# The first 24 of 72 expert tiles run between the links of the last chunk's attention chain, and twelve row buffers stand in for eight

## The chip, the core and the metric

One core of one Trainium2 chip runs the whole kernel. The metric is the time of one execution on the device in microseconds (us), as the median of several runs. The engines of the core are TensorE (PE in the profile, its weight loads PEld), VectorE (DVE), ScalarE (ACT), GpSimd (POOL) and SyncE (SP, which here only issues DMAs). Each works through its own queue strictly in order, and they meet through semaphores.

## The reference

The input is x of 4 x 1024 tokens of 128 channels. Two layers follow, each with attention and a feed-forward part and a layernorm behind each of the four:

```python
x = _layernorm(x + _L0_attn_ref(x, L0_attn_w_qkv, L0_attn_w_out), axis=-1)
x = _layernorm(x + _L0_ffn_ref(x, ...), axis=-1)
x = _layernorm(x + _L1_attn_ref(x, L1_attn_Wq, L1_attn_Wk, L1_attn_Wv, L1_attn_Wo), axis=-1)
x = _layernorm(x + _L1_ffn_ref(x, L1_ffn_W_gate, L1_ffn_W_in, L1_ffn_b_in, L1_ffn_W_out, L1_ffn_b_out), axis=-1)
```

The last one is the part that the change is about. It is a mixture of 8 experts with the 2 best for each token:

```python
gate_logits = jnp.einsum('bpd,de->bpe', x, W_gate)
top_w, top_idx = jax.lax.top_k(gate_logits, K)
top_w = jax.nn.softmax(top_w, axis=-1)
...
for e in range(E):
    h = jax.nn.gelu(jnp.einsum('bpd,dm->bpm', x, W_in[e]) + b_in[e], approximate=False)
    y = jnp.einsum('bpm,md->bpd', h, W_out[e]) + b_out[e]
    out = out + combine[..., e, None] * y
```

## The kernel before

**Stages.** The first attention runs head group by head group until about 540 us (the last of its exponentials starts at 540.2). Then `rear` (L873) runs the rest in chunks of 128 tokens of each of the 4 batches (512 tokens), 8 chunks in all. `body` (L483) is the program of one iteration. It is cut into three parts: "pre" (the output projection of the first attention and its layernorm), "front" (the first feed-forward part) and "rear" (the second attention, its layernorm, the gate and the routing). In iteration `it` the part "rear" is at chunk it-2, the other two are ahead. Iterations 0 and 1 have no rear part; 2 to 7 are a loop; iteration 8 has front and rear, and iteration 9, the last, has the rear part alone (L900 to L910). All engines go through the same written order; a class `Tape` (L353) gives each operation its semaphore values and hands out the 8 PSUM banks in turn (`bank`, L423).

**The end of the rear part.** Behind the last attention step comes `project1(0)` and `project1(1)` (L719: 32 matmuls each, and one add on VectorE at L725), then layernorm 3 (`layernorm`, L458: statistics, variance, a power on GpSimd at L466, the normalization at L469), a transpose and its copy (`turned`, L472), the gate's matmuls (L778), the choice of two experts on VectorE and one exponential on ScalarE (`choose`, L775), the counting matmuls (L810, L812) and `route` (L802), which gives each token and choice a row in the DRAM tensor `rows`, where each expert has a region of its own. `base` holds the next free row of each expert. Then GpSimd issues 8 scatters with one indirect DMA each (L855). The plain result goes to `best` as the residual (L759).

**The experts.** `experts` (L914) follows the last iteration. `tile_table` (L1085) has 16 dependent VectorE steps that find, from `base`, how many tiles of 128 rows each expert has, and for each of 72 tiles (`NTILE`) its expert and its first row. SyncE and ScalarE fill up the last tile of each expert with padding rows, four DMAs each (L924). SyncE waits for all padding and for all scatters (L928 to L931), and then all engines meet at L933. A tile then goes through this pipeline: SyncE reads its row number from the table and loads 128 rows of 130 words (`load`, L949); TensorE transposes (`turn`, L954), VectorE copies the transpose (`take_x`, L986) and the expert's 128 x 640 weights (`take_w`, L991), TensorE has 4 matmul calls (`up`, L959), ScalarE 4 Gelus (`gelu`, L977), TensorE 4 more calls (`down`, L969; an f32 matmul call shows as two matmuls), VectorE scales the bias (`weigh`, L1006) and forms the result (`take_y`, L998), and GpSimd adds it into `best` with one indirect DMA (`back`, L1012). TensorE's order for tile j is turn(j+3), up(j+1), down(j); VectorE's is take_x(j+3), take_w(j+2), weigh(j+1), take_y(j). A row buffer `x_g[k]` is used again when `back` of the tile in it has landed; there are `XG` = 8. The first 8 tiles are written out, the next 56 are a loop of 8 tiles, the last 8 are written out again.

**The tail.** When all of `back` has landed, `best` is read in 8 pieces, the two choices are added, the last layernorm is made and the result is stored (L1040 to L1083).

## Time and profile before

| what | value |
|---|---|
| median of 3 runs | 1412.0 us (1405.41 to 1414.06) |
| profiled execution, its own time | 1410.33 us |
| its span | 1408.2 us |
| mean granted TensorE clock | 0.956 of full speed |
| first scatter of the last chunk starts | 1208.74 us |
| first `back` starts | 1235.14 us |
| last `back` starts | 1377.78 us |

All times from the trace count from the start of the span, which is 2.1 us shorter than the execution's own time. In a timeline row stand the start, the length, the engine, the line and the operation, and in brackets how long the engine had been idle before, with what ended it. A line in a helper, such as L450, L466 or L469, serves several places, so those rows are told apart by their time.

### The profile page before, as it was taken

What the parts mean: (1) busy time and instruction counts of PE and PEld (TensorE: products, weight loads), DVE (VectorE), ACT (ScalarE), POOL (GpSimd) and SP (SyncE); (2) the same over time, 40 slices, a digit from 0 to 9 for tenths busy, and PEclk for the clock granted to TensorE, in tenths of its full rate; (3) what the DMA queues carried; (4) which work ended last, traced back from release to release, by engine and by line L of the source; (5) the groups of instructions that cost most, each with busy time, mean ns of one, the idle gap of its engine ahead of it and who ended that gap; (6) DMA issues with size and microseconds to landing.
All of it is one profiled execution on the core that took longest, in us unless ns stands there. A gap on an engine that the chain in (4) does not pass through costs nothing. (4 is left out here: it accounts for less than half of the span.)

```text
span 1408.2 us, 45352 instructions
## 1 busy us (share of the span) xinstructions
PE 1244.9 (88%) x16752; PEld 764.5 (54%) x16753; DVE 943.2 (67%) x1984; ACT 660.6 (47%) x1321; POOL 518.2 (37%) x509
## 2 busy tenths in 40 slices
PE   7589999999999978999999999999999967299990
PEld 4244444444444433457475656556465635199990
DVE  5668888788877842276867767685868556456664
ACT  4256676666766664242425252333324231055554
POOL 7311211212112211032534436161534344278785
PEclk9789999999999998999999999999999988599995
DMA  6453112121121223030404031131303050244555
GB/s 194 125 190 106 49 47 61 51 58 48 48 61 53 58 75 122 29 76 25 103 16 109 0 84 41 41 84 32 98 7 90 9 156 2 53 58 63 67 63 187
DMA packets 95006, 99.91 MB, mean 71 GB/s; under 512 B 16096, under 2 KB 76640, under 8 KB 94752
## 3 DMA queue, kind: packets, MB, share of 16 engines
q1 hardware_dynamic: 75808, 81.47, 20.6%
q0 software_dynamic: 13568, 12.13, 5.5%
q10 hardware_dynamic: 5504, 4.46, 1.0%
q8 instruction: 99, 1.62, 0.5%
q14 instruction: 27, 0.22, 0.0%
HBM read 49.84 MB, written 27.87 MB: 55 GB/s over the span
## 5 line engine op out<-in xcount | busy, mean ns | idle before, releaser
L1487 DVE TENSOR_REDUCE arena<-banks 128x4 f32<-128x512 f32 (+3 forms) x336 | 343.7, 1068 | 94.7 <-PE banks L1256 90.3
L1422 ACT ACTIVATE arena<-banks 128x512 f32<-128x512 f32 x576 | 304.9, 603 | 166.0 <-PE banks L1256 160.9
L1256 PE MATMUL banks<-arena 99*32 99x512 bf16 (+7 forms) x6144 | 337.0, 331 | 30.3 <-DVE arena L1487 12.1
L1256 PEld LDWEIGHTS banks<-arena 96*32 96x32 bf16 (+1 forms) x6144 | 151.4, 97 | 191.2 <-ACT arena L1422 69.3
L450 PE MATMUL banks<-arena,h 128*128 128x512 f32 x512 | 226.7, 593 | 2.4 <-DVEq L395 1.0
L1624 POOL TENSOR_SCALAR_AFFINE_SELECT arena<-arena 128x512 f32<-128x512 f32 x128 | 79.9, 637 | 383.1 <-ACT arena L1422 369.7
L1323 PE MATMUL banks<-arena 128*32 128x512 f32 (+3 forms) x1536 | 153.7, 490 | 11.2 <-POOL arena L1624 11.0
L450 PEld LDWEIGHTS banks<-arena,h 128*128 128x128 f32 x512 | 94.7, 190 | 110.0 <-issue 105.2
L598 ACT ACTIVATE arena<-banks,sh 128x512 f32<-128x512 f32 x64 | 44.0, 687 | 215.9 <-PE banks L450 215.9
L1015 POOL DMA_INDIRECT best<-arena x72 | 117.4, 1630 | 42.8 <-issue 25.8
L466 POOL TENSOR_TENSOR arena<-arena 128x4 f32<-128x4 f32 x23 | 23.4, 1017 | 267.0 <-DVE arena L464 267.0
L637 POOL TENSOR_TENSOR arena<-arena,qdec 128x512 f32<-128x512 f32 x64 | 87.6, 1391 | 63.5 <-DVE arena L541 43.1
L982 ACT ACTIVATE arena<-banks,b_in 128x128 f32<-128x128 f32 x288 | 82.3, 369 | 61.2 <-PE banks L964 55.2
L1256 PE MATMUL banks<-mask_qk,identb 128*32 128x128 bf16 x2048 | 102.9, 222 | 1.9 <-issue 1.9
L586 POOL TENSOR_TENSOR arena<-arena,kdec 128x512 f32<-128x512 f32 x64 | 84.5, 1345 | 32.8 <-ACT arena L577 17.6
L712 DVE SCALAR_TENSOR_TENSOR arena<-arena,bdec,banks 128x128 f32<-128x128 f32 x256 | 69.0, 342 | 30.6 <-PE banks L699 30.6
L855 POOL DMA_INDIRECT rows<-arena x64 | 63.5, 993 | 49.3 <-DVE arena L829 25.8
L450 PE MATMUL banks<-h,arena 128*128 x576 | 80.0, 282 | 1.4 <-ACT arena L982 0.8
L964 PE MATMUL banks<-arena 128*128 128x128 f32 x576 | 78.9, 281 | 2.1 <-DVE arena L995 2.1
L708 ACT COPY arena<-banks 128x512 f32<-128x512 f32 x64 | 34.4, 590 | 89.7 <-PE banks L699 89.7
L964 PEld LDWEIGHTS banks<-arena 128*128 128x128 f32 x576 | 71.6, 195 | 3.4 <-issue 2.7
L450 PEld LDWEIGHTS banks<-h,arena 128*128 128x128 f32 x576 | 69.8, 191 | 3.6 <-issue 2.3
(172 smaller groups left out, 1761.5 us busy)
## 6 DMA issues: line engine op xcount, KB each, us to landing
arena<-arena SPq DMA_DIRECT2D x160, 128.0 KB, 2.3
arena<-k_parts SPq DMA_DIRECT2D x96, 96.0 KB
arena<-rows SPq DMA_DIRECT2D x72, 65.0 KB
arena<-q_parts SPq DMA_DIRECT2D x64, 64.0 KB
k_parts<-arena SPq DMA_DIRECT2D x24, 128.0 KB, 3.2
q_parts<-arena POOLq DMA_DIRECT2D x24, 128.0 KB, 3.0
arena<-q_parts SPq DMA_DIRECT2D x32, 96.0 KB
best<-arena SPq DMA_DIRECT2D x12, 256.0 KB, 3.0
```

The lines of the kernel that those rows point to most:

```text
L450: ins = nc.tensor.matmul(dst, l, r, start=(n == 0), stop=(n == len(pairs) - 1), skip_group_check=True)
L586: lambda: nc.gpsimd.tensor_tensor(v_dec[:, n % 2, kp, :, :].rearrange("p g (i d) -> p g i d", i=4), v_nat[:, n, 2 * kp:2 * kp + 2, :].rear ...
L637: lambda: nc.gpsimd.tensor_tensor(q_dec[:, n % 2, 4 * kp:4 * kp + 4, :, :], q_all[:, 4 * kp:4 * kp + 4, n * P:(n + 1) * P].rearrange("p i ...
L712: tp.do("dve", f"state{n}", [f"attn{n}", f"grow{n}"], lambda: last(nc.vector.scalar_tensor_tensor(out=state[:, 2 * pr:2 * pr + 2, blk, :], ...
L964: ins = nc.tensor.matmul(banks[:, 2 + k % 2, m * P:(m + 1) * P], w_now[:, k % 4, m * P:(m + 1) * P], x_gT[:, k % 4, :], start=True, stop=T ...
L982: ins = nc.scalar.activation(h_g[:, k % 2, m * P:(m + 1) * P], banks[:, 2 + k % 2, m * P:(m + 1) * P], ACT.Gelu, bias=b_in[:, bass.ds(x, 1 ...
L1015: nc.gpsimd.indirect_dma_start(out=best, out_offset=bass.IndirectOffsetOnAxis(x_g[:, k, C:C + 1].bitcast(U32), 0), in_=y_g[:, k, :], in_of ...
L1256: ins = nc.tensor.matmul(dst[c:c + 32, :], lhs[:, c:c + 32], rhs, start=start, stop=stop, skip_group_check=True)
L1323: done.append(nc.tensor.matmul(pv_bank[32 * h:32 * h + 32, lo:lo + n], va[p][:, kt, h, :], pe_[:, s % NSLOT, at:at + n], start=(g in (0, 3 ...
L1422: nc.scalar.activation(pe_[:, s % NSLOT, :], score[s % NBANK], ACT.Exp, scale=SCALE0)\
L1487: nc.vector.tensor_reduce(mx[:, 1 if k0 else 0, qt, hs[0]:hs[-1] + 1], src, AX.X, ALU.max)\
L1624: ins = nc.gpsimd.affine_select(out=v, in_=v, compare_op=ALU.is_ge, fill=0.0, base=0, pattern=[[0, v.shape[1]], [1, P]], channel_multiplie ...
```

## The change

- `XG` goes from 8 to 12. `h_g` moves to the memory of `k_all`, since the row buffers now fill `q_all`.
- The first 24 tiles (`AHEAD`) are planned by a new function `plan_table` of 19 dependent VectorE steps in iteration 8, behind its layernorm 3. It uses `base` after six chunks and counts only tiles that are full by then. Their loads need the scatters of the first six chunks alone.
- The steps of a tile are in a class `Tiles`. In the last iteration, behind `project1(0)`, `begin` issues on SyncE the 12 first loads, on TensorE three transposes and on VectorE three `take_x`, two `take_w` and one `weigh`. From there the rear part has only PSUM banks 6 and 7 (`narrow`), and TensorE waits first for the users of the other six.
- Four tiles are run by `slot(0)` to `slot(3)` between the links of the rear part: most of slot 0 between the power and the normalization of layernorm 3, slot 1 behind the normalization, slot 2 behind the transpose, slot 3 between `choose` and `route`. Tiles 4 to 23 are written out behind the rear part.
- `tile_table` now has 21 steps for the other 48 tiles, in three parts behind tiles 5, 7 and 9 on VectorE. All eight padding DMAs are on SyncE, two each behind its steps for tiles 6 to 9. The waits for all scatters, for the padding and for the table are at tile 24, and the meeting of all engines is gone. SyncE's order is load(j+12) in the slot of tile j.
- The first `back` waits for the zeroing of `best` and for the plain result of the last chunk (L759).
- The other 48 tiles are a loop of 12 tiles that runs three times, and 12 written out.

```diff
-XG = 8
+XG = 12
+AHEAD = 24
+LATER = NTILE - AHEAD
...
@@ body
             project1(0)
+            if tp.tiles:
+                tp.tiles.begin(tp)
...
+            if tp.tiles:
+                tp.tiles.first_up()
-            layernorm(tp, 3, "res3_1", res, x3, [("scatter7", 1), ("stored", 1)])
+            layernorm(tp, 3, "res3_1", res, x3, [("scatter7", 1), ("stored", 1)], lambda: slot(0, "sp", "pe", "act", "dve"))
+            slot(0, "y", "pool")
+            slot(1, "sp", "pe", "act", "dve")
+            if tp.me == "dve" and tp.eng is not None and isinstance(it, int) and it == NITER - 2:
+                tp.wait(("base", 1))
+                tp.wait(("outproj", 1))
+                plan_table()
...
             tile2(2)
             tp.part = "rear"
+            slot(1, "y", "pool")
+            slot(2, "act")
             turned(tp, 3, x3, x3T, [("gate", 1), "up_b3"])
...
+            slot(2, "sp", "pe", "dve", "y", "pool")
             choose()
+            slot(3, "sp", "pe", "act", "dve", "y", "pool")
...
@@ Tiles
+                def load(J, k):
+                    if isinstance(J, int) and XG * J + k == AHEAD:
+                        e.wait_ge(s_line["scat"], 16 * TOPK * B * (NITER - 2))
+                        e.wait_ge(s_pad, 16 * 2 * NE)
...
+                def back(J, k):
+                    if isinstance(J, int) and XG * J + k == 0:
+                        e.wait_ge(s_zeroed, 16 * (NZERO - NT // 512))
+                        e.wait_ge(s_line["out"], 16 * NITER)
...
+            def begin(self, tp):
+                e, me = self.e, self.me
+                owed = tp.narrow()
+                if me in ("sp", "act", "dve"):
+                    tp.wait("scores3")
+                    tp.wait("qdec31")
...
+                if me == "sp":
+                    e.wait_ge(s_line["scat"], 16 * TOPK * B * (NITER - 4))
+                    for j in range(XG):
+                        self.do("load", j)
+                if me == "pe":
+                    for n in owed:
+                        tp.wait(n)
+                    for j in range(3):
+                        self.do("turn", j)
...
@@ experts
+            table_parts = tile_table() if me == "dve" else iter(())
+            for j in range(4, AHEAD):
+                tiles.slot(j, ("sp", "pe", "act", "dve", "y", "pool"))
+                if j in (5, 7, 9):
+                    next(table_parts, None)
+                if me == "sp" and j in (6, 7, 8, 9):
...
-            e.sem_inc(s_off, 1)
-            e.wait_ge(s_off, 10)
```

## Rows read from the trace of the kernel before

**Rows 1.** The chain of waits, ahead of the tiles and behind them.
```profile
1213.57 6.93 issue
...
1377.78 3.23 DMA best<-arena
```

**Rows 2.** The costliest groups of the page, line 1015.
```profile
L1015 POOL DMA_INDIRECT best<-arena x72 | 117.4, 1630 | 42.8 <-issue 25.8
```

**Rows 3.** Line 1015 by itself (ns least/median/most), then its timeline.
```profile
L1015 POOL DMA_INDIRECT best<-arena x72: 1549/1602/1870, 1235.1 to 1377.8; - x72
...
1235.14 1.67 POOL L1015 DMA_INDIRECT best<-arena  x1 [15.97 <-DVE arena L1002]
...
1267.40 1.55 POOL L1015 DMA_INDIRECT best<-arena  x1 [1.05 <-DVE arena L1002]
```

**Rows 4.** Timeline of TensorE, the transposes of two tiles that follow each other.
```profile
1235.68 0.27 PE L957 MATMUL banks<-ident,arena 128*128 128x128 f32 x1
...
1237.57 0.27 PE L957 MATMUL banks<-ident,arena 128*128 128x128 f32 x1
```

**Rows 5.** The chain of waits, a back that lands and the load that follows it.
```profile
1256.98 3.37 DMA best<-arena
1260.51 3.02 DMA arena<-rows
```

**Rows 6.** Line 855 in the last chunk, the eight scatters (ns).
```profile
L855 POOL DMA_INDIRECT rows<-arena x8: 957/970/1264, 1208.7 to 1218.2; - x8
```

**Rows 7.** Timeline of VectorE: the gap in iteration 8, and the table's first and last step.
```profile
1132.40 0.19 DVE L781 COPY arena<-banks 128x32 f32<-128x32 f32 x1 [7.69 <-PE banks L778]
...
1207.83 0.17 DVE L1101 CAST arena<-arena 128x8 uint32<-128x8 f32 x1
...
1214.14 0.20 DVE L1117 CAST arena<-arena 128x72 uint32<-128x72 f32 x1
```

**Rows 8.** Timeline of SyncE's queue: four padding DMAs, then four loads.
```profile
1209.04 4.54 SPq L924 DMA_DIRECT2D rows<-in_padding  x4
1221.37 3.65 SPq L952 DMA_DIRECT2D arena<-rows  x4
```

**Rows 9.** Timeline of TensorE: one gate, a projection, the last gate, a tile's up.
```profile
1131.41 0.95 PE L778 MATMUL banks<-wgate,arena 128*128 128x8 f32 x8
...
1194.47 1.95 PE L450 MATMUL banks<-wo1s,arena 128*128 128x128 f32 x16
...
1202.23 1.87 PE L778 MATMUL banks<-wgate,arena 128*128 128x8 f32 x8 [0.68 <-ACTq L395]
...
1233.89 1.06 PE L964 MATMUL banks<-arena 128*128 128x128 f32 x8
```

**Rows 10.** Timeline of VectorE, the links of the last chunk's rear part.
```profile
1192.34 0.42 DVE L725 TENSOR_TENSOR arena<-banks,arena 128x256 f32<-128x256 f32 x1 [1.58 <-PE banks L450]
...
1198.24 0.17 DVE L464 TENSOR_SCALAR arena<-arena 128x4 f32<-128x4 f32 x1
1199.56 1.11 DVE L469 TENSOR_SCALAR arena<-arena 128x128 f32<-128x128 f32 x4 [1.15 <-POOL arena L466]
...
1206.61 0.23 DVE L816 TENSOR_TENSOR arena<-banks,arena 128x72 f32<-128x72 f32 x1
```

**Rows 11.** Timeline of VectorE in the tiles, from a take_x to the next weigh.
```profile
1286.58 0.28 DVE L989 COPY arena<-banks 128x128 f32<-128x128 f32 x1
...
1287.82 0.28 DVE L1010 TENSOR_SCALAR arena<-arena 128x128 f32<-128x128 f32 x1
```

**Rows 12.** Timeline of ScalarE: the exponential, then the first Gelus of the tiles.
```profile
1205.53 0.21 ACT L790 ACTIVATE arena<-arena 128x4 f32<-128x4 f32 x1 [3.34 <-DVE arena L788]
...
1230.21 1.28 ACT L982 ACT_TABLE_LOAD   x1 [24.48 <-PE banks L964]
1231.51 2.18 ACT L982 ACTIVATE arena<-banks,b_in 128x128 f32<-128x128 f32 x8
```

**Rows 13.** Busy time in one stretch: span, PE, PEld, DVE, ACT, POOL, granted TensorE clock, DMA share, GB/s.
```profile
1202.00:1207.00 5.00, 2.38 (x17) 2.19 (x17) 2.48 (x24) 0.39 (x2) 0.00 (x0) 0.50 0.11 33
```

More of the change, by code:

```diff
@@ L365, in __init__ @@
                 self.part = None
+                self.tiles = None
+                self.two = None
             def wait(self, need):
@@ L421, in do, with narrow @@
                 self.where[name] = (line, self.count[line])
-            def bank(self):
+            def narrow(self):
+                last = {}
+                for k in range(len(self.held)):
+                    last[k % 8] = self.held[k]
+                self.two = [last[6], last[7]]
+                self.turn = 0
+                return [n for b in range(6) for n in last[b]]
+            def bank(self):
+                if self.two is not None:
+                    if self.part not in self.live:
+                        return None, banks[:, 6, :], []
+                    self.turn ^= 1
+                    return -1 - self.turn, banks[:, 6 + self.turn, :], self.two[self.turn]
                 k = len(self.held)
@@ L486, in body, with slot @@
             c = it - 2
+            def slot(j, *who):
+                if tp.tiles:
+                    tp.tiles.slot(j, who)
             tp.part = "pre"
@@ L893, in rear, with run @@
             body(dry)
-            def run(it, live):
+            def run(it, live, tiles=None):
                 tp = Tape(e, me, it, live, dry)
+                tp.tiles = tiles
                 body(tp)
@@ L909, in rear @@
                 e.dma_start(w_dn, a["w_dn"].rearrange("e p m c -> p e (m c)")).then_inc(s_experts, 16)
-            run(NITER - 1, {"rear"})
-            experts(e, me)
-        def experts(e, me):
-            if me == "dve":
-                tile_table()
-            if me in ("sp", "act"):
-                e.wait_ge(s_tab, 1)
-                for g in range(NE):
-                    if g % 2 == (me == "act"):
-                        r = e.value_load(table[0:1, 2 * NTILE + g:2 * NTILE + g + 1], min_val=0,
+            tiles = Tiles(e, me)
@@ new lines, in experts @@
+        def experts(e, me, tiles):
+            table_parts = tile_table() if me == "dve" else iter(())
[4 more added lines that the diff above has]
+                if me == "sp" and j in (6, 7, 8, 9):
+                    if j == 6:
+                        e.wait_ge(s_tab, 1)
+                    for g in range(2 * j - 12, 2 * j - 10):
+                        r = e.value_load(table[0:1, 2 * LATER + g:2 * LATER + g + 1], min_val=0,
@@ L949, in load @@
-            def load(J, k):
-                r = e.value_load(at(NTILE + XG * J + k), min_val=0, max_val=NE * REGION + NE * P - P)
-                wait(s_back[k], 16 * J)
-                e.dma_start(x_g[:, k, :], rows[bass.ds(r, P), :]).then_inc(s_xg[k], 16)
-            def turn(J, k):
-                e.wait_ge(s_xg[k], 16 * (J + 1))
-                wait(s_xt, XG * J + k - 1)
-                nc.tensor.transpose(banks[:, k % 2, 0:P], x_g[:, k, 0:C], ident[:, :]).then_inc(s_tp, 1)
-            def up(J, k):
-                e.wait_ge(s_xt, XG * J + k + 1)
-                e.wait_ge(s_w1, XG * J + k + 1)
-                wait(s_gelu, XG * J + k - 1)
-                for m in range(4):
-                    ins = nc.tensor.matmul(banks[:, 2 + k % 2, m * P:(m + 1) * P],
-                                           w_now[:, k % 4, m * P:(m + 1) * P],
-                                           x_gT[:, k % 4, :], start=True, stop=True, skip_group_check=True)
-                ins.then_inc(s_up, 1)
@@ L1012, in back @@
-            def back(J, k):
-                e.wait_ge(s_y, XG * J + k + 1)
-                e.sem_inc(s_hold, 1)
-                nc.gpsimd.indirect_dma_start(
-                    out=best, out_offset=bass.IndirectOffsetOnAxis(x_g[:, k, C:C + 1].bitcast(U32), 0),
-                    in_=y_g[:, k, :], in_offset=None, compute_op=ALU.add).then_inc(s_back[k], 16)
-            chain = {"sp": [(load, 0)], "pe": [(turn, 3), (up, 1), (down, 0)], "act": [(gelu, 0)],
-                     "dve": [(take_x, 3), (take_w, 2), (weigh, 1), (take_y, 0)], "pool": [(back, 0)]}[me]
@@ L1022, in experts, with group @@
             NJ = NTILE // XG
-            for fn, ahead in chain:
-                for k in range(ahead):
-                    fn(0, k)
-            def tiles(J, final):
+            def group(J, final):
                 for k in range(XG):
-                    for fn, ahead in chain:
+                    for fn, ahead in tiles.chain:
                         if k + ahead < XG:
@@ L1033, in tiles @@
                             fn(J + 1, k + ahead - XG)
-            tiles(0, False)
-            with e.Fori(1, NJ - 1) as J:
-                tiles(J, False)
-            tiles(NJ - 1, True)
+            with e.Fori(AHEAD // XG, NJ - 1) as J:
+                group(J, False)
+            group(NJ - 1, True)
             NC = 2 * B
```

257 lines of the change are left out of this document (181 added, 76 removed).

## The prediction

> **What bounds the kernel now.** I read the chain of waits first. Between the last step of the rear part at about 1208 us and the first `back` at 1235.14 it holds no matmul work of weight: a table, 6.93 us of nothing but waiting for scatters [rows 1], and then the pipeline of the first tile. Behind that stand the tiles, and behind them a tail from 1377.78 on. The group of line 1015 says what bounds the tiles: 72 indirect DMAs of 1.63 us mean with the engine idle 0.30 us at least between two of them, that is 1.93 us for a tile on GpSimd [rows 2, 3]. TensorE needs nearly as much: two transposes that follow each other start 1.89 us apart with no idle row between them [rows 4]. The 72 starts run from 1235.14 to 1377.78, so the real pitch is 142.64 / 71 = 2.01 us [rows 3]. The 0.08 above GpSimd's own 1.93 are places where it waits for its feed, such as the 1.05 us at 1267.40 [rows 3]: a load that could go only when the `back` of eight tiles earlier had landed [rows 5].
>
> So two things are to be had: the 26.4 us from the first scatter at 1208.74 [rows 6] to the first `back`, in which GpSimd has only 8 scatters to issue, and some of the 0.08 us a tile.
>
> **The plan, its loads and the memory.** `plan_table` has 19 steps where the table of before took 1207.83 to 1214.34 for 16 [rows 7], most of them wider. 19 x (6.51 / 16) = 7.7 us is the upper end; its widest steps have 256 elements where the old ones had 576, and I take 5. VectorE is idle 7.69 us at that place of iteration 8 [rows 7], so it costs 0; above the cover it would cost 0 to 1. SyncE has nothing else to do there: its 12 loads at 1.10 us (3.65 us for four, less one issue) [rows 8] can start once the scores of the last step have left `q_all`, some 8 us before TensorE wants the first. Free too.
>
> **What the four tiles cost the rear chain.** Let T be the end of `project1(1)`, 1196.42 before [rows 9]. TensorE now waits for the add behind `project1(0)`, done at 1192.76 [rows 10], since its bank is one of the six handed over, and then has three transposes, the third behind a VectorE copy: some 1.3 us. T becomes 1197.8, which is 1.4 later.
>
> From there, in us behind T. Before: variance done 2.0, normalized 4.3, gate done 7.7, `place` behind the counting matmuls at 10.2, first scatter 12.3 [rows 6, 9, 10].
> - VectorE has a take_x, a take_w and a weigh in the place where it waited 1.15 us for the power [rows 10]. They take 1.52 us in the tiles, from 1286.58 to 1288.10 [rows 11]. Normalized at 4.7.
> - ScalarE needs the Gelu table, 1.28 us [rows 12], between up(0) and the first Gelu: gelu(0) ends at 3.7 and gelu(1) at 4.8, at half of 2.18 us each [rows 12].
> - TensorE, in order: up(0), turn(3), up(1), down(0) to 4.7, turn(4), up(2), down(1) to 6.8, at 0.95 us for an up or a down that is not held up (half of the 1.89 [rows 4]). Only then the transpose of x3, whose input lay ready at 4.7: done 7.2, copied 7.9.
> - turn(5), up(3), down(2) to 9.2, and the gate to 10.2. It takes 0.95 us at the full 2.4 GHz; before it took 1.87, with a granted clock of 0.50, that is 1.2 GHz, after a stretch in which TensorE had had one transpose since T [rows 9, 13]. The tiles keep TensorE busy there, so I take 0.95.
> - The choice up to the exponential is 1.4 us, as from 1204.10 to 1205.53 [rows 9, 12]: the exponential ends at 11.8. Before, slot 3 was not there. Now gelu(3) is behind the exponential, with the Gelu table once more: 13.2, done 14.4; down(3) 15.3. The counting matmuls are behind down(3), with VectorE behind take_y(3): 15.9. From `place` to the first scatter it is 2.1 us as before, 1206.61 to 1208.74 [rows 6, 10].
>
> First scatter at T + 18.0 instead of T + 12.3, so 5.7 + 1.4 = 7.1 us later: 1215.8. The lower end is 3: only what waits of `begin` and one Gelu with its table. The upper end is 14.7: TensorE at 1.2 GHz all through, where an up of 1.06 takes about twice that, 1.9 us more for each of four tiles. I take 7.1, since TensorE has no gap of over 3 us in this plan.
>
> Here the Trainium skill speaks against the change: "ScalarE: Activation LUTs", section "What ACT_TABLE_LOAD costs", gives a switch of table set 2.66 us, of which 1.28 are the load and the rest a drain. The trace has the load at 1.28, and the first Gelu starts 0.02 us behind it [rows 12]. By the page the two switches on the chain would add 2 x 1.38 = 2.8 us, which I leave out.
>
> **What the tiles gain.** GpSimd has `back` 0 to 3 done before the scatters: 0 when the plain result has landed (about T + 8), 3 at T + 15.7 to 17.3, just free for the first scatter. Then 8 scatters, mean 1.04 + 0.30 [rows 6], 10.7 us: `back` 4 starts at 1226.5. By then TensorE is six tiles ahead, so GpSimd has work without a gap, and its queue alone sets the pace: 67 x 1.93 = 129.3. The last `back` starts at 1355.8 instead of 1377.78: **22.0 us earlier**. The tail stays.
>
> Does the feed hold? Twelve buffers give 12 x 1.93 = 23.2 us for a round that takes, from the start of a `back`, 3.4 + 3.0 to the landed load [rows 5], four TensorE slots of 1.89 and a take_y, together some 15. The three parts of the table add about 2 us each on VectorE between tiles 5 and 10, while GpSimd is still at the scatters: covered by the six tiles. On SyncE each of the slots 6 to 9 has two padding DMAs at 1.30 behind its load of 1.10 [rows 8], 3.7 us against a pitch of 1.93, so it falls 7 us behind. The tightest load, of tile 22, is then issued by 1249.9 and its result is there at about 1260, while GpSimd wants it at 1226.5 + 18 x 1.93 = 1261.2. It holds by 1 us; were it missed, by a microsecond or two once.
>
> Bounds of the pace: 1.85 (1.55 + 0.30, the least) makes it 5.4 us better; the pitch of before, 2.01, makes it 5.3 worse. I take 1.93, the mean of all 72 rows.
>
> **The sum.** The profiled execution has 1410.33 us; less 22.0 it is 1388.3. The median shown, 1412.0, is 1.7 above the profiled one, so I predict 1390.0 for the median. The forecast's own range is 1380 to 1398.
>
> **The rivals.**
> 1. *The pitch does not fall.* The feed sets it and not GpSimd: TensorE at 1.89 is only 0.04 below, and 2.01 is what a tile took [rows 3, 4]. For it: GpSimd's idle time is 25.8 / 70 = 0.37 us a row and not 0.30 [rows 2], the longer waits left out. Against: twelve buffers and a lead of six tiles, which at 0.08 a tile would last to the end. Gain 22.0 - 5.3 = 16.7: 1395.
> 2. *GpSimd is held up more.* Its rows range from 1.55 to 1.87 [rows 3]. If all were 1.87, because it now never rests and always meets VectorE's copies, 67 x 0.24 = 16 us are lost: gain 6, 1406. Against: 70 of 72 rows had tile work on VectorE beside them and the mean is 1.63. "SBUF — State Buffer", section "Who interferes with whom", of the Trainium skill says that VectorE in a two-port mode and GpSimd lock each other out for a whole instruction; the spread of 0.32 us over rows of one shape agrees with that, and no row here says how often it will fall so.
> 3. *The slots do not fit the chain*, the slower side. In each slot every engine does a tile's step ahead of the next link, and the one waits for the other. Run one after the other, a tile's steps are 11 us (from the first load's issue at 1221.37 to the first `back` at 1235.14 are 13.8 [rows 3, 8], of which I give the load some 2.5); four of them, 44 us, would put the first scatter at 1252.7 and the end 15 us later than before: 1427. It decides from 29 us of delay on (7.1 + 22.0). Against: steps of two tiles are always in the queue, and TensorE's part of four tiles is 7.6 us.
> 4. *It does not do what it says*: `back` 0 to 3 come only behind the scatters, since the plain result is late or GpSimd is at the wrong place. Then four more of 1.93 stand behind them: gain 14.3, 1397.
> 5. *Better:* the chain loses only 3 us, or the pace is 1.88: gain 26, 1386 and below.
>
> **How the numbers follow.** Forecast 0.57, rival 1 0.16, rival 2 0.09, rival 3 0.03, rival 4 0.05, rival 5 0.10. A measurement of this kernel tells about 1%, 14 us, from no change. Faster by over 1% (below 1397.9) are the forecast, rival 5, nearly all of rival 1 and half of rival 4: 0.84. Slower by over 1% is rival 3 alone: 0.03. Within 1%: 0.13. From 1377 to 1400 lie the forecast, rivals 1 and 5 and most of rival 4; it leaves out rivals 2 and 3.
>
> **What would show it.** Right: four rows of `back` ahead of the first scatter of the last chunk; the first scatter at about 1216; 8 scatters in 10 to 11 us; then 68 rows of `back` with an idle time of 0.30 nearly throughout and a last start near 1356; the gate at 0.95 us; two table loads more on ScalarE; no 6.93 us of pure waiting. Wrong: a first scatter behind 1225, gaps on GpSimd over 1 us at tiles 20 to 24 (SyncE's padding), a mean `back` above 1.75, or TensorE at half clock between 1192 and 1216.

## The result, and the profile after

| | before | after |
|---|---|---|
| median | 1411.22 us (7 runs, 1405.41 to 1414.06) | 1401.75 us (7 runs, 1398.41 to 1403.32) |
| profiled execution, its span | 1410.33, 1408.2 us | 1403.32, 1401.6 us |
| A, the add behind the projection in iteration 8 (VectorE) | 1120.48 | 1123.89 |
| first scatter of the last chunk | 1208.74 = A + 88.3 | 1221.43 = A + 97.5 |
| last `back` starts | 1377.78 = A + 257.3 | 1371.43 = A + 247.5 |

The ratio of the mean times is 0.9937, with a 95% interval of 0.9915 to 0.9958. By the medians the change is 9.5 us faster where 22 were forecast, and 1401.75 is outside the range. A lies ahead of everything that the change touches in the timeline, and from one profiled execution to the next it lies anywhere from 1115.5 to 1123.9 us with the same code ahead of it, so I count from A. By that the last `back` is 9.8 us earlier, and not 22.0.

GpSimd in the last chunk, from its timeline; line 1066 is `back` and line 906 the scatters. The first row shown is `back`(0), the second `back`(3); dots stand for rows left out:

```profile
1209.07 1.64 POOL L1066 DMA_INDIRECT best<-arena  x1 [4.29 <-DVE arena L1050]
...
1219.39 1.73 POOL L1066 DMA_INDIRECT best<-arena  x1 [4.94 <-POOLq L407]
1221.43 1.00 POOL L906 DMA_INDIRECT rows<-arena  x1 [0.30 <-issue]
...
1230.56 1.08 POOL L906 DMA_INDIRECT rows<-arena  x1 [0.30 <-issue]
1231.95 1.60 POOL L1066 DMA_INDIRECT best<-arena  x1 [0.30 <-issue]
...
1236.87 1.77 POOL L1066 DMA_INDIRECT best<-arena  x1 [1.45 <-DVE arena L1050]
...
1249.44 1.56 POOL L1066 DMA_INDIRECT best<-arena  x1 [2.70 <-DVE arena L1050]
...
1257.23 1.62 POOL L1066 DMA_INDIRECT best<-arena  x1 [0.50 <-issue]
...
1371.43 1.55 POOL L1066 DMA_INDIRECT best<-arena  x1 [0.30 <-issue]
```

Four tiles are done ahead of the scatters, as planned. The scatters take 10.5 us, from 1221.43 to 1231.95. Against the prediction the last `back` is 12.2 us late (A + 247.5 for A + 235.3), and these rows split that into three:
- first scatter at A + 97.5 where the sum gave 95.3: 2.2 us (the scatters themselves gave 0.2 back);
- tiles 4 to 13, from 1231.95 to 1257.23: 25.3 us for nine steps, where nine of 1.93 are 17.4: **7.9 us**. GpSimd waits for VectorE's take_y (line 1050) before tiles 6, 8, 9, 10, 11 and 12;
- the other 58 steps, 114.2 us, at 1.97 and not 1.93: 2.3 us.

The group of line 1066 answers to [rows 2]. A `back` costs what it did; the idle time before it hardly fell:

```profile
L1066 POOL DMA_INDIRECT best<-arena x72 | 116.3, 1615 | 41.4 <-issue 22.8 <-DVE arena L1050 13.7 <-POOLq L407 4.9
```

The timeline of TensorE answers to [rows 9] and goes on to the waits. Lines: 481 down, 825 the gate, 857 and 859 the counting, 1005 turn, 1012 up.

```profile
1210.49 0.96 PE L825 MATMUL banks<-wgate,arena 128*128 128x8 f32 x8
...
1211.44 1.06 PE L1012 MATMUL banks<-arena 128*128 128x128 f32 x8
1216.13 2.07 PE L481 MATMUL banks<-h,arena 128*128 x8 [3.63 <-ACT arena L1030]
...
1218.07 0.46 PE L859 MATMUL banks<-arena 128*128 128x64 bf16 x8
...
1223.21 1.06 PE L481 MATMUL banks<-h,arena 128*128 x8
...
1224.21 1.06 PE L1012 MATMUL banks<-arena 128*128 128x128 f32 x8
1225.10 1.14 PE L481 MATMUL banks<-h,arena 128*128 x8
...
1230.92 2.05 PE L1012 MATMUL banks<-arena 128*128 128x128 f32 x8 [4.57 <-issue]
1232.79 2.07 PE L481 MATMUL banks<-h,arena 128*128 x8
```

The gate has its 0.96 us. Then come two gaps, each followed by matmuls of twice the length: 3.63 us ahead of down(3) and 4.57 us ahead of up(8). What follows the first is at 1.2 GHz, by the granted clock (0.50) of that stretch, the row that answers to [rows 13]:

```profile
1216.00:1220.00 4.00, 3.87 (x25) 3.81 (x26) 1.65 (x10) 1.03 (x4) 0.61 (x1) 0.50 0.08 21
```

In the first gap TensorE waits for ScalarE, which has the exponential, its way back to the Gelu table and gelu(3), as [rows 12] had them for the tiles:

```profile
1212.86 0.21 ACT L837 ACTIVATE arena<-arena 128x4 f32<-128x4 f32 x1 [1.99 <-DVE arena L835]
1213.56 1.28 ACT L1030 ACT_TABLE_LOAD   x1 [0.49 <-issue]
1214.85 2.18 ACT L1030 ACTIVATE arena<-banks,b_in 128x128 f32<-128x128 f32 x8
```

At the second gap, VectorE and ScalarE (line 1050 take_y, 1239 the first step of the table's first part, 1043 take_w, 1030 the Gelus) have these rows:

```profile
1227.07 0.35 DVE L1050 SCALAR_TENSOR_TENSOR arena<-banks,arena 128x128 f32<-128x128 f32 x1 [2.79 <-PE banks L481]
1227.33 0.16 DVE L1239 CAST arena<-arena 128x8 uint32<-128x8 f32 x1
...
1230.32 0.49 DVE L1043 COPY arena<-arena 128x640 f32 x1 [0.67 <-issue]
...
1235.72 0.35 DVE L1050 SCALAR_TENSOR_TENSOR arena<-banks,arena 128x128 f32<-128x128 f32 x1 [4.71 <-PE banks L481]
```
```profile
1231.51 1.14 ACT L1030 ACTIVATE arena<-banks,b_in 128x128 f32<-128x128 f32 x4 [6.86 <-remote]
1235.95 1.14 ACT L1030 ACTIVATE arena<-banks,b_in 128x128 f32<-128x128 f32 x4 [3.30 <-PE banks L481]
```

Read them pairwise with TensorE's. down(5) is over at 1224.27 (1223.21 + 1.06), yet take_y(5), which VectorE stands idle for, starts at 1227.07. up(7) is over at 1225.27, and its Gelu, with ScalarE idle for 6.86 us, starts at 1231.51. down(6) is over at 1226.24, and take_y(6) starts at 1235.72, VectorE having been idle for 4.71 us. So what TensorE has done by its records reaches the other engines 3 to 10 us later. It is not the waiting engine that is slow: gelu(8) waits for down(6) as well, as the user of its buffer, and it starts on ScalarE at 1235.95, 0.23 us behind take_y(6) on VectorE. Nor is it the loading of program code, as far as the trace shows: the instruction queues moved no packet between 1218 and 1236 us. Behind the late take_y(5) stand a table part and take_w(8), and behind that up(8): the gap of 4.57 us.

### The profile page after: what moved, and what is told of

The parts are those of the page before. It is cut to its first block and busy times, and to the rows that moved or that the text cites. A ratio compares the mean times of both kernels' runs of the same rounds, so it can differ in the third digit from the quotient of the medians.

```text
span 1401.6 us, 45150 instructions
## 1 busy us (share of the span) xinstructions
PE 1246.2 (89%) x16752; PEld 767.7 (55%) x16753; DVE 951.1 (68%) x2008; ACT 662.7 (47%) x1323; POOL 516.9 (37%) x509
## 5 line engine op out<-in xcount | busy, mean ns | idle before, releaser
L1635 DVE TENSOR_REDUCE arena<-banks 128x4 f32<-128x512 f32 (+3 forms) x336 | 343.4, 1066 | 92.8 <-PE banks L1404 88.4
L481 PE MATMUL banks<-h,arena 128*128 x576 | 83.0, 290 | 5.9 <-ACT arena L1030 5.3
L1012 PEld LDWEIGHTS banks<-arena 128*128 128x128 f32 x576 | 74.3, 202 | 11.1 <-issue 10.8
L481 PEld LDWEIGHTS banks<-h,arena 128*128 128x128 f32 x576 | 74.0, 201 | 7.3 <-issue 6.8
```

Source lines behind the costliest of these rows:

```text
L481: ins = nc.tensor.matmul(dst, l, r, start=(n == 0), stop=(n == len(pairs) - 1), skip_group_check=True)
L1012: ins = nc.tensor.matmul(banks[:, 2 + k % 2, m * P:(m + 1) * P], w_now[:, k % 4, m * P:(m + 1) * P], x_gT[:, k % 4, :], start=True, stop=T ...
L1635: nc.vector.tensor_reduce(mx[:, 1 if k0 else 0, qt, hs[0]:hs[-1] + 1], src, AX.X, ALU.max)\
```

## The experiments

Each group of runs below is one session on one chip; groups 1 and 5 had the same chip, groups 2, 3 and 4 one each of their own; that of the first result is not on record. The unedited changed kernel, repeated as a control, does not have one time: 1401.75 at first, then 1391.06 (group 2), 1397.13 (group 3), 1390.46 (group 4) and 1393.12 us (group 5). "Nine steps" is the time from `back`(4) to `back`(13); where tiles start behind the scatters it is the first `back` behind them and the nine that follow. "Later pitch" is the mean step from there to the last `back`. These and the times behind A come from the one profiled execution of each row, which need not lie at its median.

| run | median us | ratio to before, 95% | first scatter | nine steps | later pitch | last `back` |
|---|---|---|---|---|---|---|
| before | 1411.22 | | A + 88.3 | 17.5 | 2.02 | A + 257.3 |
| the change | 1401.75 | 0.9915–0.9958 | A + 97.5 | 25.3 | 1.97 | A + 247.5 |
| e1 unedited | 1390.9 (one run) | | A + 97.4 | 18.4 | 1.97 | A + 240.4 |
| e2 buffers alone | 1404.09 | 0.9971–0.9997 | A + 87.7 | 17.2 | 1.98 | A + 253.8 |
| e3 table in seven parts | 1394.13 | 0.9875–0.9920 | A + 97.7 | 17.2 | 1.98 | A + 240.0 |
| e4 tiles behind scatters | 1396.70 | 0.9903–0.9941 | A + 87.4 | 20.8 | 2.02 | A + 243.7 |
| e5 unedited | 1391.06 | 0.9853–0.9895 | A + 97.5 | 18.4 | 1.97 | A + 240.4 |
| e6 Gelu first | 1386.61 | 0.9812–0.9846 | A + 93.2 | 17.5 | 1.97 | A + 236.0 |
| e7 = e6 + e3 | 1389.62 | 0.9825–0.9870 | A + 94.9 | 17.2 | 1.98 | A + 237.4 |
| e8 = e4 + seven parts | 1396.21 | 0.9866–0.9910 | A + 89.3 | 22.3 | 1.97 | A + 244.4 |
| e9 unedited | 1397.13 | 0.9883–0.9927 | A + 97.3 | 24.9 | 1.97 | A + 246.9 |
| e10 Gelu first | 1395.70 | 0.9879–0.9939 | A + 93.6 | 25.2 | 1.97 | A + 243.2 |
| e11 half of down | 1391.59 | 0.9838–0.9890 | A + 95.6 | 22.3 | 1.87 | A + 236.9 |
| e12 unedited | 1390.46 | 0.9856–0.9913 | A + 97.1 | 18.7 | 1.97 | A + 240.4 |
| e13 scatters later | 1398.67 | 0.9919–0.9964 | A + 122.3 | 17.3 | 1.91 | A + 245.5 |
| e14 filled, 32 | 1393.91 | 0.9875–0.9917 | A + 99.3 | 16.8 | 1.98 | A + 241.6 |
| e15 tiles behind scatters | 1397.54 | 0.9894–0.9942 | A + 88.3 | 20.1 | 2.04 | A + 245.4 |
| e16 unedited | 1393.12 | 0.9851–0.9905 | A + 96.0 | 18.4 | 1.97 | A + 239.0 |
| e17 scatters later | 1398.16 | 0.9885–0.9937 | A + 122.6 | 17.2 | 1.90 | A + 245.3 |
| e18 filled, 12 | 1391.23 | 0.9823–0.9882 | A + 96.9 | 16.9 | 1.97 | A + 238.4 |

### Group 1: the parts of the change

e1 is the changed kernel as it is.

> The changed kernel once more, with nothing edited, to see whether the gaps behind the scatters are a property of it. In its first profile tiles 4 to 13 took 25.3 us on GpSimd where nine pitches of 1.93 are 17.4, and two up/down groups of TensorE signalled up to 6 us after their matmuls in the record. Theory (the VectorE queue starves the feed): 1399 to 1403 us and 24 to 27 us for those nine pitches again. Rival (a chance stall of TensorE in that one execution): the late signals are gone and the nine pitches take 20 us or less.

It gave 1390.9 us in its one execution, 10.9 below the first result, and the table shows where: the nine steps take 18.4 us and not 25.3. First scatter and later pitch are the same. So the largest of the three losses is not in the program alone.

e2, the kernel before with twelve row buffers and nothing else:
```diff
-XG = 8
+XG = 12
-        x_gT, h_g = reuse([P, 4, P]), reuse([P, 2, 512])
+        x_gT, h_g = reuse([P, 4, P]), k_all
```

> The kernel of before with 12 row buffers and nothing else. If the 0.08 us a tile above GpSimd's own 1.93 come from the loads that wait for a buffer, the pitch falls from 2.01 to 1.93 to 1.95 and the time by 4 to 5 us (ratio 0.996 to 0.997). If they come from somewhere else (TensorE at 1.89 with VectorE's steps between), the pitch stays at 1.98 to 2.01 and the ratio is 0.998 to 1.001.

The pitch behind the first ten tiles falls from 2.02 to 1.98, the last `back` comes 3.5 us sooner, and the ratio is 0.9984. That is the second of the two outcomes expected: the buffers do not bring GpSimd to 1.93. They are worth 2.2 us by the ratio of the means (0.4 to 4.1) and 3.5 by the medians, and their pitch ends where that of the changed kernel ends, at 1.97 to 1.98.

e3, a piece of three steps of the table behind each of tiles 4 to 10:
```diff
-                if j in (5, 7, 9):
+                if 4 <= j <= 10:
```

> The changed kernel with the 21 steps of the table in seven parts of three behind tiles 4 to 10, not in three parts behind tiles 5, 7 and 9. The work is the same. Theory (a part of 2 us at a time on VectorE holds take_w and take_y of the next tile, and the feed starves): the nine pitches fall from 25 to 20 to 22 us and the ratio to before from 0.994 to 0.990. Rival (the gaps come from TensorE at 1.2 GHz and late, or from SyncE's padding): no change, 0.993 to 0.995.

Against e1 the nine steps are 1.2 us shorter and the last `back` 0.4 us earlier: nearly nothing. The 25 us that the expectation starts from did not occur in e1, so it was not tried as written. Where completions come in time, the parts of 2 us on VectorE are nearly covered, as was forecast.

e4, all 24 planned tiles behind the scatters, nothing between the links:
```diff
-                if tp.tiles:
-                    tp.tiles.slot(j, who)
+                pass
-            for j in range(4, AHEAD):
+            for j in range(0, AHEAD):
```
(`begin` and `first_up` move to the end of `body`.)

> The changed kernel with nothing between the links: begin, first_up and tiles 0 to 3 stand behind the route of the last chunk, and the tiles run from there on. The plan, the 12 buffers and the table parts stay. By the sum of the prediction the four slots gain 4 x 1.93 = 7.7 us of GpSimd's queue and cost 7.1 to 9 us of delay of the first scatter, so this kernel is as fast as the changed one or up to 2 us faster from that alone; and since TensorE builds up its lead over GpSimd while the scatters go out, with the table inside that lead, up to 8 us more come back: ratio 0.985 to 0.993. Rival (the slots are where the gain of the change is): 0.996 to 1.000.

The chain keeps its old length (A + 87.4), the first `back` comes with no wait behind the last scatter, at 1214.57, and the end is only 3.3 us behind e1's. So most of the change's gain, 13.6 of 16.9 us by the last `back`, is what it does behind the scatters (tiles planned ahead, the buffers, the table off the path); the four tiles between the links add the rest. That profile is the fastest of e4's four runs. By the medians of group 4, where e15 repeats it, the parts are 11.1 of 18.1 us. The ratio of 0.9922 is in the range expected (0.985 to 0.993), but the expectation also took e4 to be as fast as the change or faster, and it is slower. The four tiles between the links cost the chain 10 us and bring four tiles of 1.9 plus TensorE's lead. Without the lead GpSimd waits, at tiles 8 and 10 most:

```profile
1233.17 1.71 POOL L1064 DMA_INDIRECT best<-arena  x1 [2.33 <-DVE arena L1048]
...
1239.63 1.56 POOL L1064 DMA_INDIRECT best<-arena  x1 [2.70 <-DVE arena L1048]
```

### Group 2: the exponential and the Gelu table

e5, unedited, five rounds:

> The changed kernel unedited, now timed in five rounds beside the kernel before on one chip. Its first seven runs gave 1401.75 us against 1411.22 (0.9937), one run on another chip 1390.9 against 1407.6 (0.988). If the late signals of TensorE belong to that first chip or execution, this is 0.986 to 0.990 here, with the nine pitches behind the scatters at 18 to 19 us. If they belong to the kernel and come and go, the runs spread over 1390 to 1403 and the ratio is about 0.991.

1391.06 us. The nine steps again take 18.4 us. The same place in GpSimd's timeline, to be laid beside the first fence:

```profile
1225.02 1.60 POOL L1066 DMA_INDIRECT best<-arena  x1 [0.31 <-DVE arena L1050]
...
1241.25 1.71 POOL L1066 DMA_INDIRECT best<-arena  x1 [1.10 <-DVE arena L1050]
```

And TensorE's down(5), up(8) and down(7), then VectorE's take_y(5):

```profile
1216.31 1.06 PE L481 MATMUL banks<-h,arena 128*128 x8
...
1221.23 1.26 PE L1012 MATMUL banks<-arena 128*128 128x128 f32 x8 [1.86 <-issue]
1222.28 2.00 PE L481 MATMUL banks<-h,arena 128*128 x8
```
```profile
1217.40 0.35 DVE L1050 SCALAR_TENSOR_TENSOR arena<-banks,arena 128x128 f32<-128x128 f32 x1 [0.27 <-PE banks L481]
```

down(5) is over at 1217.37, and take_y(5) starts at 1217.40. The gap ahead of up(8), which waits for the take_w behind the table part, is 1.86 us where it was 4.57; down(7) behind it still takes 2.00 us. The order of the program, the gap ahead of down(3), the half clock behind it and the table part are the same in both executions; what differs is how late TensorE's completions arrive.

e6 puts gelu(3) ahead of the exponential on ScalarE:
```diff
+            slot(3, "act")
             choose()
-            slot(3, "sp", "pe", "act", "dve", "y", "pool")
+            slot(3, "sp", "pe", "dve", "y", "pool")
```

> ScalarE does the Gelus of tile 3 ahead of the exponential of the gate and not behind it; nothing else is moved. The prediction gave that place 1.3 us for the second table load and 1.1 for the Gelus, behind which down(3) and the counting matmuls wait, and the trace shows 3.63 us of TensorE idle there and half clock after it. Theory (this wait is the largest single link of the 12 us by which the scatters come later): first scatter 4 to 5 us earlier, time 3 to 5 us below the changed kernel on the same chip. Rival (the feed behind the scatters takes it back): first scatter earlier, time within 1 us of the changed kernel.

ScalarE's timeline: gelu(3), the exponential's table (1.28 us, over well before its input is there), the exponential, and the Gelu table again, now for tile 4:

```profile
1204.03 1.14 ACT L1031 ACTIVATE arena<-banks,b_in 128x128 f32<-128x128 f32 x4 [0.40 <-PE banks L1013]
1205.19 1.28 ACT L837 ACT_TABLE_LOAD   x1
1207.00 0.21 ACT L837 ACTIVATE arena<-arena 128x4 f32<-128x4 f32 x1 [0.53 <-DVE arena L835]
1208.00 1.28 ACT L1031 ACT_TABLE_LOAD   x1 [0.79 <-PE banks L481]
```

First scatter 4.3 us sooner than in e5, last `back` 4.4 us sooner, median 4.5 us lower, and the ratio's interval lies below that of e5: 1386.61 us, the lowest median of all.

e7 (e6 with the table in seven parts) and e8 (e4 with it):

> e6 with the table in seven parts of three steps behind tiles 4 to 10. If the parts of 2 us held the feed, this is 1 to 3 us below e6, since with earlier scatters there is less lead to hide them; if they did not, it is equal to e6.

> e4 (no tile between the links) with the table in seven parts of three steps behind tiles 0 to 6. In e4 GpSimd waited 8 us in all at tiles 6 to 11, each time for VectorE. Theory (the table's steps in VectorE's queue): those waits fall to under 2 us and the time 4 to 7 us below e4, so that running behind the chain beats running between its links: 1389 to 1392. Rival (TensorE has simply no lead there): the waits stay and so does the time.

Neither gained: 1389.62 us against e6's 1386.61, with intervals that overlap, and 1396.21 against 1396.70 for e4, which ran in the other session. In e8 the waits of 2.3 and 2.7 us at tiles 8 and 10 are gone, but 0.5 to 1.6 us stand at each of tiles 1 to 8, 7.7 us in sum against 8.4 in e4. Spreading the table moves the waits and does not shorten them.

### Group 3: the late completions again

> The changed kernel unedited for the third time, five rounds. It gave 0.9937 of before in its first seven runs and 0.9874 in e5, with a profile that has late TensorE signals of up to 6.1 us at tiles 5 to 7 in the first case and none in e1 and e5. If the slower result belongs to one chip or one session, this is 0.986 to 0.990 again unless it meets the same chip. If it comes and goes in the kernel, some of these runs lie at 1398 to 1403 and others at 1390.

> e6 once more in another session beside the unedited changed kernel, as the version that may beat it: 3 to 5 us below it again if the place of the Gelus of tile 3 is what counts; within 1 us if e6 was a matter of that session.

Here the losses of the first profile are back, for both kernels: nine steps of 24.9 and 25.2 us. In e9, VectorE's take_y and ScalarE's Gelu at the same tiles:

```profile
1223.64 0.35 DVE L1050 SCALAR_TENSOR_TENSOR arena<-banks,arena 128x128 f32<-128x128 f32 x1 [3.32 <-PE banks L481]
1232.27 0.35 DVE L1050 SCALAR_TENSOR_TENSOR arena<-banks,arena 128x128 f32<-128x128 f32 x1 [4.69 <-remote]
```
```profile
1229.46 1.14 ACT L1030 ACTIVATE arena<-banks,b_in 128x128 f32<-128x128 f32 x4 [8.65 <-remote]
```

e10 keeps e6's earlier first scatter (3.7 us, A + 93.6) and its earlier last `back` (3.7 us), though the medians are only 1.4 us apart here, with intervals that overlap.

One suspect for the late completions falls with e10: TensorE's gap ahead of down(3) and the half clock behind it. e10 has no such gap. From 1198 us until turn(10) is over at 1216.57 TensorE never stands idle for more than 1.70 us, and it has its full clock until 1218 (granted clock 1.00). Its rows of up(7) and down(6), the clock, gelu(7), and take_y(6) (the lines are one higher here):

```profile
1214.51 1.06 PE L1013 MATMUL banks<-arena 128*128 128x128 f32 x8
1215.41 1.06 PE L481 MATMUL banks<-h,arena 128*128 x8
...
1198.00:1218.00 20.00, 15.14 (x133) 14.18 (x132) 13.30 (x64) 12.06 (x34) 11.54 (x10) 1.00 0.29 51
...
1222.85 1.14 ACT L1031 ACTIVATE arena<-banks,b_in 128x128 f32<-128x128 f32 x4 [7.94 <-PE banks L1013]
...
1227.05 0.35 DVE L1051 SCALAR_TENSOR_TENSOR arena<-banks,arena 128x128 f32<-128x128 f32 x1 [6.88 <-PE banks L481]
```

up(7) is over at 1215.57 and down(6) at 1216.47, and their followers start 7.3 and 10.6 us later. So neither the gap ahead of down(3) nor a half clock behind it is needed for the late completions. The scatters are still beside them. In the first profile, in e9 and in e10 take_y(6) starts 14.3 us behind the start of the first scatter, while the recorded end of down(6) lies 4.8, 4.3 and 3.7 us behind it. This points at the scatters and does not show that they are the cause. (e11, below, also has late completions, at tiles 6 to 8.)

e11 leaves out two of down's four matmul calls, so that half of the hidden columns are missing from the result:
```diff
-                         for m in range(4)]).then_inc(s_down, 1)
+                         for m in range(2)]).then_inc(s_down, 1)
```

> The changed kernel with two of the four down matmul calls of each tile, so the second half of the hidden columns is left out of the result. TensorE's pace falls from 1.89 to about 1.45 us a tile, GpSimd's work is untouched. Behind tile 13 the changed kernel takes 1.97 us a tile where GpSimd alone would need 1.91 (1.61 + 0.30). If that 0.06 is TensorE's and the lead that it lacks, the pitch falls to 1.91 to 1.93 and the time by 4 to 6 us; if it is GpSimd's own (code, DMA), the pitch stays at 1.96 to 1.98 and only the first tiles gain, 1 to 2 us.

It takes 1391.59 us, 5.5 below e9. The pitch falls to 1.87, lower than the 1.91 to 1.93 expected, with GpSimd's `back` at a median of 1.551 and a mean of 1.57:

```profile
L1066 POOL DMA_INDIRECT best<-arena x72: 1549/1551/1792, 1208.6 to 1359.7; - x72
```

That is 1.57 + 0.30, GpSimd's own pace. In the unedited kernel TensorE sets 1.97. TensorE's rows of e5 between 1243 and 1357 us, by line, say so as well:

```profile
L481 PE MATMUL banks<-h,arena 128*128 x464 | 63.7, 280 | 0.5 <-DVE arena L1050 0.5
L1012 PE MATMUL banks<-arena 128*128 128x128 f32 x448 | 59.8, 277 | 0.1
```

0.6 us idle in 114. Yet the last 50 starts of a transpose that I could pair lie 1.98 us apart on average, 1.89 to 2.34: the step of 1.89 that [rows 4] show is the least and not the mean. The trace of the kernel before says the same of its TensorE, busy for 92.61 of 93.00 us in the middle of the tiles:

```profile
1257.00:1350.00 93.00, 92.61 (x779) 89.88 (x778) 57.95 (x184) 52.26 (x184) 74.79 (x46) 1.00 0.50 66
```

### Groups 4 and 5: what makes the completions late?

Two suspects lie beside tiles 5 to 7: the scatters that run on GpSimd meanwhile, and TensorE's gap with the half clock behind it. e10 speaks against the second, as said above; these runs were to try both.

> The changed kernel unedited once more, as the control of the three beside it. If its time depends on the chip by TensorE's late completion signals, either the ten backs behind the scatters take about 18 us and the run is near 1390 us, or they take 25 us with DVE's take_y of tiles 5 to 7 idle on PE for several us, and the run is near 1398 us. A time of 1398 us with 18 us for the ten backs would put the difference between chips elsewhere.

e13 and e17 move the scatters behind `back`(11):
```diff
+            if tp.tiles and tp.me == "pool":
+                for j in range(4, 12):
+                    slot(j, "pool")
             for g in range(TOPK * B):
```

> The eight scatters of the last chunk come behind back(11) in place of back(3), so that GpSimd's scatters lie beside tiles 12 to 20 and not beside tiles 5 to 10. If GpSimd's scatters are what holds TensorE's signals back, the late signals (where this chip has them) move to tiles 12 and later or go, and take_y of tiles 5 to 7 waits under 0.5 us. If the place in the program or the half-clock stretch before it sets them, they stay at tiles 5 to 7. Price: the lead in tiles is used up before the scatters and not after, so backs 4 to 11 run at TensorE's and VectorE's pace (about 2 us each) and the time is 0 to 5 us above the control where signals are in time.

e14 and e18 fill TensorE's gap ahead of down(3) with matmuls into a bank that is overwritten:
```diff
                 def down(J, k):
                     x = expert_of(XG * J + k)
+                    if isinstance(J, int) and J == 0 and k == 3:
+                        wait(s_y, XG * J + k - 1)
+                        for n in range(32):
+                            nc.tensor.matmul(banks[:, 5, 0:P], ident[:, :], ident[:, :], start=True, stop=True,
+                                             skip_group_check=True)
```

> 32 matmuls of 128 columns into an unused bank fill TensorE's idle 3.6 us ahead of down(3); their results are overwritten. If TensorE's idle time and half clock before tiles 5 to 7 bring the late signals on, they go or fall to under 1 us where this chip has them, and the time is about 7 us below the control. If the clock has nothing to do with it, the ten backs behind the scatters stay at the control's time within 1 us. Where there are no late signals at all, only down(3) can gain (1 us at full clock in place of 2.07) or lose up to 1 us behind the last of the added matmuls.

> Tiles begun only behind the last scatters, on this chip. If the late signals come with the tiles' first ten steps wherever these lie, GpSimd waits some 7 us more here than the 8 us of the run before; if they come with matmuls of the tiles beside running scatters, there are none here, since no tile has begun while the scatters run, and the time is within 2 us of 1396.7, that is under the control's where the control has late signals.

This chip has no late completions (18.7 us for the nine steps of e12), and neither had the next (18.4 in e16). So the scatters could not be tried, and the cause of the late completions stays open. The runs tell other things.

*e13* has 1398.67 us, 8.2 above e12 where 0 to 5 were expected.

*The 32 matmuls were mis-sized.* They took 7.31 us, 0.228 each, where I had reckoned with less than 3.6 in all. The first scatter came 2.2 us later than the control's, and the nine steps were 1.9 us shorter.

*e15* has 1397.54 us, 7.1 above its control, as e4 was above e1. Whether it would have been free of late completions on a chip that has them was not tried.

> The changed kernel unedited, the control of the two beside it. Either near 1390 us with about 18.5 us for nine steps of the backs behind the scatters (signals in time), or 1396 to 1402 us with about 25 us for them and take_y of tiles 5 to 7 waiting on PE for several us (signals late).

> Scatters behind back(11). Where the control's signals are late: they stay at tiles 5 to 7 if the place in the program or the half clock brings them on, and move to tiles 12 and later, or go, if the running scatters do. In time or not, the backs from tile 12 on follow each other at 1.91 us and not 1.97, as in the run before this one: with the scatters behind tile 11 TensorE has its lead back, and the waits at tiles 26, 36 to 43, 48 and 49 are gone. Backs 4 to 11 wait about 12 us in sum, and the time is about 8 us above a control with signals in time.

e17 has the pitch that was expected, 1.90 for 1.91, and is 5.0 us above e16 where about 8 were expected. Its waits of line 1069 (`back` there) behind the scatters, from 1248 to 1361 us:

```profile
POOL best L1069 <- issue: 15.8, 52, 0.3
POOL best L1069 <- DVE arena L1053: 2.4, 8, 0.3
```

No wait over 0.31 us for 60 tiles, and a pitch of 1.90. With eight scatters at tile 12, TensorE gains a lead of some 10 us there, and GpSimd lives off it to the end. So GpSimd can go at 1.90; at 1.97 it has used the lead up and follows TensorE.

> 12 added matmuls, 2.7 us at the 0.228 us that each of the 32 took, inside the 3.6 us gap ahead of down(3). Half clock as the cause: down(3) takes 1.06 and not 2.07 us, the half-clock stretch behind it is gone, late signals are gone where the control has them, and the first scatter comes 1 us (with the transposes and matmuls behind it up to 2 us) earlier than in the control. Clock without effect: first scatter and backs as in the control within 0.5 us.

TensorE in e18, the added matmuls (line 1022) and down(3):

```profile
1209.66 2.84 PE L1022 MATMUL banks<-ident 128*128 128x128 f32 x24
1213.46 1.15 PE L481 MATMUL banks<-h,arena 128*128 x8 [0.96 <-ACT arena L1035]
```

down(3) takes 1.15 and not 2.07 us. From the start of the gate to the first scatter it is 9.95 us (1207.82 to 1217.77) against 10.94 in e16 (and 10.76 to 10.94 in every unedited run): the half clock costs the chain 1.0 us, and the nine steps behind it 1.5 us. From A to the gate this execution was 1.9 us slower than e16's, which no added matmul explains, so the last `back` is only 0.6 us earlier by A; the medians are 1.9 us apart, with intervals that overlap.

## Why the prediction was wrong

**Right, and within a microsecond.** `plan_table` costs nothing: its 19 steps run from 1128.02 to 1133.25, 5.2 us where 5 were taken, inside the gap of [rows 7]:

```profile
1128.02 0.16 DVE L1207 TENSOR_TENSOR arena<-arena,region 128x8 f32<-128x8 f32 x1
...
1133.08 0.17 DVE L1226 TENSOR_TENSOR arena<-arena 128x8 f32<-128x8 f32 x1
```

The end of `project1(1)` came 1.8 us later (1.4). The gate had its full clock. The scatters took 10.5 us (10.7), a `back` 1.62 us (1.63). SyncE's padding held nothing up: the rows of tiles 14 to 24 have no wait over 0.5 us. The drain that the Trainium skill, "ScalarE: Activation LUTs", section "What ACT_TABLE_LOAD costs", adds to a load of 1.28 us was rightly left out: the load at 1213.56 is over at 1214.84 and gelu(3) starts at 1214.85. Rival 4 fell, rival 3 fell (10 us of delay for the four slots and not 29), rival 2 fell.

**The step that failed** is "By then TensorE is six tiles ahead, so GpSimd has work without a gap". It cost 7.9 us of the missing 12.2. The lead is not six tiles. In e5, where completions come in time, `back`(4) starts at 1225.02 and down(7) is over at 1224.28: the results of four tiles are ready. By the rows the half clock behind the gap at down(3) and the gap of 1.86 us behind the first table part had taken the rest. In the execution of the result `back`(4) starts at 1231.95, and the results of two tiles are ready, 4 and 5; take_y(6) comes at 1235.72. What GpSimd needs is not work issued on TensorE but the chain of signals from TensorE to ScalarE and back and to VectorE, and here these came 3 to 10 us behind the matmuls' recorded ends at tiles 5 to 7, with up(8) behind them.

Where they come in time, in four of six sessions, the nine steps take 18.4 to 18.7 us, 1.0 to 1.3 over the sum; so 6.6 to 6.9 of the 7.9 us are the late completions. Three of these sessions have ratios: 0.9874, 0.9885 and 0.9878, which is 16 to 18 us of gain by the means and 18 to 20 by the medians. Their medians of 1390.5 to 1393.1 lie near the 1390.0 forecast, but that is in part luck. The last `back` is 17 to 18 us earlier there and not 22, the mechanism has the same faults, and the kernel before had medians of 1408.6 to 1412.2 beside them. That the session makes a difference is shown by the repeats of one and the same kernel, each with a single execution profiled; the single runs of e9 (from 1394.70) and of e16 (up to 1396.92) overlap. What in the chip does it is not shown.

**The half clock.** "TensorE has no gap of over 3 us in this plan" was wrong by its own figures: it had the gate done at T + 10.2 and down(3) not before T + 14.4, with one transpose and one up, some 1 us, between them. TensorE fell to half clock behind it, down(3) took 2.07 and not 0.95 us, and `place` (line 863, at 1218.56) came 1.0 us late by the sum. `back`(3), behind the late take_y, held GpSimd until 1221.12, so the first scatter came 2.9 us behind `place` and not 2.1. With the 0.4 us of `project1(1)` these are the 2.2 us of the first term. e18 takes the half clock away and gets 1.0 of it back; e6 takes the whole place out of the chain and gets 4.3.

**The pace.** "Its queue alone sets the pace: 67 x 1.93" took TensorE's least step, 1.89, for its mean, 1.98. In the changed kernel TensorE sets the pace, as e11 shows. In the kernel before it is busy for all but 0.4 of 93 us in the tiles as well, and e2 ends at the same 1.98, but neither was tried with less work on TensorE. GpSimd's own pace is 1.87 to 1.90 (e11, e17). This is rival 1's mechanism at under half its price: 2.3 us here.

By e4 and e15 the larger part of the gain comes from what the change does behind the scatters, which the prediction had not priced apart. The best version is e6, the change with gelu(3) ahead of the exponential: 0.9829 (0.9812 to 0.9846). In the session with late completions its median was 1.4 us below the control's, which the noise covers.

## What to carry to other kernels

Where two engines are within a few per cent of each other, take the mean step of each over many tiles, not the shortest, and test the claim by making one of them cheaper. Before work is put between the links of a chain, write down each engine's order and look for a switch (here of ScalarE's table) that leaves TensorE idle: moving one Gelu ahead of the exponential brought the last `back` forward by 4.4 us in one session and 3.7 in another. And repeat a result on other chips before its mechanism is explained: the largest loss here came and went with the session.

## What the hardware showed that was not expected

In two of six sessions TensorE's completions reached VectorE and ScalarE 2 to 11 us behind the recorded ends of the matmuls, in each of the four executions profiled there (the first one, e9, e10, e11). It was always at the tiles beside the last chunk's scatters (tiles 5 to 8), for some 12 us, and then no more; in the e9 rows a Gelu stands idle for 8.65 us. It came in e10 with the full clock too. Whether the signal was late or the matmul itself, with its record too early, the trace can't tell; two engines that wait for the same matmul start 0.2 us apart, so it is no delay of the waiting engines. Elsewhere in the same executions a follower with nothing else to wait for starts within 0.2 us, and the later pitch of 1.97 is the same in all sessions.
